# Layer-norm moments moved to ScalarE and the graph products started one tile earlier

## The reference

```python
xn = _layernorm(x)                       # (x - mean) / sqrt(var + 1e-5) over the 768 features of a token
x = x + gnn(xn, src, dst) + mix(xn)      # two graph attention layers; a linear-attention block with MLP
x = x + ffn(_layernorm(x))               # experts chosen by a router

# inside gnn
x_norm = layer_norm(xn, norm_g, norm_b)  # a second norm, of the normalised x
out1 = gat_conv(x_norm, src, dst, W1, ...)
out2 = gat_conv(out1, src, dst, W2, ...)
combined = concatenate([xn, out2], axis=-1)
return combined @ Wu + bu                # the first 768 rows of Wu meet xn itself
```

## Time and profile before

| what | us |
|---|---|
| median of 3 runs | 2093.31 |
| the profiled execution's own time | 2087.36 |
| its span (first to last instruction) | 2085.6 |
| PE busy | 1939.0 |
| DVE busy | 1163.6 |
| ACT busy | 624.6 |
| POOL busy | 423.9 |

### The profile page before, as it was taken

The page is one execution under the profiler, slowest core; times in us unless marked ns, Lnnn a source line. Parts: engine busy times, 40 slices in busy tenths (PEclk is TensorE's granted clock), DMA queues, the critical chain, the costliest instruction groups (busy, mean ns, idle before and its releaser), DMA issues.

```text
span 2085.6 us, 28329 instructions
## 1 busy us (share of the span) xinstructions
PE 1939.0 (93%) x10975; PEld 1836.1 (88%) x10975; DVE 1163.6 (56%) x2089; ACT 624.6 (30%) x1235; POOL 423.9 (20%) x323
## 2 busy tenths in 40 slices
PE   6799995999978899999899999999979999999995
PEld 3476895999878899888899999999969999999995
DVE  8977444888678332566743352442467344274347
ACT  2541323888677231222510010010241001010024
POOL 1000001011000233502242141330205123043120
PEclk9899997999979899999999999999989999999998
DMA  4231310111113321003321120110123011021013
GB/s 135 96 120 67 101 40 34 44 41 59 62 66 115 118 68 46 23 1 100 102 61 31 31 61 8 54 53 8 32 81 92 16 46 61 9 76 43 20 38 125
DMA packets 74476, 124.32 MB, mean 60 GB/s; under 512 B 3297, under 2 KB 45065, under 8 KB 74348
## 3 DMA queue, kind: packets, MB, share of 16 engines
q1 hardware_dynamic: 74348, 122.59, 18.2%
HBM read 97.12 MB, written 25.45 MB: 59 GB/s over the span
## 4 chain that ended last, share of the span: by engine, by line
PE 75%; DVE 8%; DMA 5%; ACT 4%; issue 3%; SPq 2%; POOL 1%; DVEq 0%; ACTq 0%; POOLq 0%
PE pb L964 24%; PE pa L603 23%; PE pb L603 11%; PE pb L755 4%; PE pb L872 2%; PE pa L742 2%; PE pa L755 2%; DMA md<-md_d 2%; PE pa L656 2%; DMA wt_d<-xu 2%; PE pb L773 1%; ACT sm L1309 1%; SPq L406 1%; DMA raw<-in_L_gnn_Wu 1%; ACT o1h L1334 1%
## 5 line engine op out<-in xcount | busy, mean ns | idle before, releaser
L1502 ACT ACTIVATE tr<-pb,V 128x418 f32<-128x418 f32 (+1 forms) x144 | 87.8, 610 | 769.1 <-PE pb L964 769.0
L964 PE MATMUL pb<-X_hi,uw_hi 128*128 128x416 f32 (+1 forms) x864 | 306.0, 354 | 6.0 <-issue 6.0
L964 PE MATMUL pb<-X_hi,uw_lo 128*128 128x416 f32 (+1 forms) x864 | 305.3, 353 | 0.0
L964 PE MATMUL pb<-X_lo,uw_hi 128*128 128x416 f32 (+1 forms) x864 | 305.3, 353 | 0.0
L603 PE MATMUL pa<-dw_hi,hh 128*125 128x384 f32 x960 | 246.4, 338 | 0.7 <-ACT tr L1502 0.7
L603 PE MATMUL pa<-dw_hi,hl 128*125 128x384 f32 x960 | 246.0, 337 | 0.0
L603 PE MATMUL pa<-dw_lo,hh 128*125 128x384 f32 x960 | 245.9, 337 | 0.0
L1968 DVE CAST hh<-tr 128x418 fp32r<-128x418 f32 (+1 forms) x144 | 115.3, 801 | 221.8 <-ACT tr L1502 221.8
L1082 POOL CAST uw_hi<-raw 128x768 fp32r<-128x768 f32 x48 | 42.5, 885 | 702.9 <-PE pb L964 611.6
L603 PEld LDWEIGHTS pa<-dw_hi,hh 128*125 128x125 f32 x960 | 172.4, 185 | 1.1 <-ACT tr L1502 1.0
L603 PEld LDWEIGHTS pa<-dw_lo,hh 128*125 128x125 f32 x960 | 172.9, 185 | 0.0
(11 more groups left out here) (359 smaller groups left out, 3581.5 us busy)
## 6 DMA issues: line engine op xcount, KB each, us to landing
raw<-in_L_mix_fc_w SPq DMA_DIRECT2D x48, 384.0 KB, 3.3
raw<-in_L_ffn_w SPq DMA_DIRECT2D x48, 384.0 KB, 3.3
md<-md_d SPq DMA_DIRECT2D x20, 610.4 KB
md_d<-mds SPq DMA_DIRECT2D x10, 610.4 KB
raw<-in_L_mix_qkv_w SPq DMA_DIRECT2D x24, 192.0 KB, 5.1
TOK<-in_x SPq DMA_DIRECT2D x10, 375.0 KB
xn_d<-TOK SPq DMA_DIRECT2D x10, 375.0 KB
xu<-in_x SPq DMA_DIRECT2D x10, 375.0 KB
```

The source lines that it names most:

```text
L964: last = nc.tensor.matmul(pb[:, j % 4, 0:n], w_[:, kk, :], x_[:, kk, o:o + n], start=(kk == 0 and q == 0), stop=(kk == KT - 1 and q == 2))
L1502: last = A_(RE[f"tr{j % 3}"][:, 0:w], pb[:, j % 4, 0:w], ACT.Identity if func == "mish" else func, bias=bias(b))
```

## The change

The moments of token tiles 0 to 5 are taken on ScalarE (`moments_of`: tiles 0 and 1 before the loop, 2 and 3 in t = 0, 4 and 5 in t = 1), by sums as in `spread_of`. VectorE takes those of tiles 6 to 9, two each in t = 4 and t = 5. The norms are now made for tiles 0 to 3 in t = 1, for 4 and 5 in t = 3, and for 6 to 9 in t = 6; the second norm's scales follow in t = 7 and 8 instead of 4 and 5. XFIRST goes from 3 to 2: transposes begin in t = 2, products in t = 3, and after tile 9 two token tiles are left instead of three. Only tile 1's sums are in `pb`. The edit, cut to its core:

```diff
-XFIRST = 3
+XFIRST = 2
+X_LOADS = ((0, 1, 2, 3), (4, 5, 6, 7), (8, 9))
+ACT_MOMENTS = 6
 def ln_tiles(t):
-    return {1: (0, 1, 2, 3), 2: (4, 5, 6, 7), 3: (8, 9)}.get(t, ())
+    return {1: (0, 1, 2, 3), 3: (4, 5), 6: (6, 7, 8, 9)}.get(t, ())
         def edge_sums(t):
-            return pb if t in (1, XFIRST) else pa
+            return pb if t == 1 else pa
 # SyncE
-                for u in ln_tiles(t - 1):
+                for u in ln_tiles(t):
                     sp.wait_ge(*at("ln_xn", u + 1))
                     sp.dma_start(xn_d[u], TOK[:, u, :]).then_inc(sem("xn_out"), 16)
             for u in range(NT - XFIRST - 2, NT):
                 graph_tile(u)
-                for k in {NT - 5: (3, 4), NT - 4: (5,)}.get(u, ()):
+                for k in {NT - XFIRST - 2: (3, 4), NT - XFIRST - 1: (5,)}.get(u, ()):
 # TensorE, edge_counts
-                    pe.wait_ge(*at("e_sb", t - 1 if t <= XFIRST + 1 else t))
+                    pe.wait_ge(*at("e_sb", t - 1 if t <= XFIRST else t))
 # ScalarE
+            def moments_of(u):
+                junk = RE["c0"][:]
+                act.wait_ge(*at(*x_landed(u)))
+                ch.link(A_(junk, TOK[:, u, :], ACT.Copy, accum_out=st[:, u, 0, 0:1]))
+                ch.link(A_(mv[:, u, 0:1], st[:, u, 0, 0:1], ACT.Copy, scale=-1.0 / D))
+                ch.link(A_(junk, TOK[:, u, :], ACT.Square, bias=mv[:, u, 0:1], accum_out=st[:, u, 0, 1:2]))
+                A_(mv[:, u, 1:2], st[:, u, 0, 1:2], ACT.Copy, scale=1.0 / D).then_inc(sem("ln_mv"), 1)
+            for u in range(2):
+                moments_of(u)
             for k in range(3):
                 page_high(PG_WU + k, wu[k][0], func=ACT.Copy)
 ...
+                for u in {0: (2, 3), 1: (4, 5)}.get(t, ()):
+                    moments_of(u)
                 if t == 1:
                     for k in range(3, KT):
                         page_high(PG_WU + k, wu[k][0], func=ACT.Copy)
-            x_out(NT - 3)
+            x_out(NT - 2)
 # VectorE, the loop
-                if ln_tiles(t - 1):
-                    token_norms(t - 1)
+                if ln_tiles(t):
+                    token_norms(t)
                 for k in {0: (0, 1, 2), 2: (3, 4, 5)}.get(t, ()):
                     page_low(PG_WU + k, wu[k])
-                if ln_tiles(t):
-                    dve.wait_ge(*at(f"x_in{t - 1}", 16 * len(ln_tiles(t))))
-                    token_moments(t)
-                if t == 4:
+                if t in (4, 5):
+                    token_moments((2 * t - 2, 2 * t - 1))
+                if t == 7:
 ...
-                if t == 5:
+                if t == 8:
 # VectorE, after the loop
-            x_low(NT - 4)
+            x_low(NT - 3)
             edge_table(NT - 1)
-            x_low(NT - 3)
             gained_page(0)
             gained_page(1)
-            graph_rows(NT - 5)
+            graph_rows(NT - 4)
             x_low(NT - 2)
```

More of the change, by code:

```diff
@@ L124, in chunk_of, with ln_group, x_landed @@
     return max(c for c, (a, n) in enumerate(CHUNKS) if a <= last)
-XFIRST = 3
+XFIRST = 2
 def x_tiles(t):
     return (t - XFIRST,) if t >= XFIRST else ()
+X_LOADS = ((0, 1, 2, 3), (4, 5, 6, 7), (8, 9))
+ACT_MOMENTS = 6
 def ln_tiles(t):
-    return {1: (0, 1, 2, 3), 2: (4, 5, 6, 7), 3: (8, 9)}.get(t, ())
+    return {1: (0, 1, 2, 3), 3: (4, 5), 6: (6, 7, 8, 9)}.get(t, ())
+def ln_group(t):
+    return len([s for s in range(t + 1) if ln_tiles(s)])
+def x_landed(u):
+    n = [u in g for g in X_LOADS].index(True)
+    return f"x_in{n}", 16 * len(X_LOADS[n])
 def step_of(i):
@@ L404, in _ @@
             for n in range(3):
-                for t in ln_tiles(n + 1):
+                for t in X_LOADS[n]:
                     sp.dma_start(TOK[:, t, :], x_t[t]).then_inc(sem(f"x_in{n}"), 16)
@@ L667, in x_transposes @@
                 else:
-                    pe.wait_ge(*at("e_sb", XFIRST + 1))
+                    pe.wait_ge(*at("e_sb", XFIRST))
                 six_transposes(pb[:, 3, :], pb[:, 2, :], TOK[:, u, :]).then_inc(sem("x_tr"), 1)
@@ L1189, in _ @@
             A_ = nc.scalar.activation
+            ch = Chain(act, sem("act_chain"))
             act.wait_ge(*at("v_tr", 1))
@@ L1220, in _ @@
             for t in range(NT):
-                tiles = ln_tiles(t - 1)
+                tiles = ln_tiles(t)
                 if tiles:
                     a, b = tiles[0], tiles[-1] + 1
-                    act.wait_ge(*at("ln_ag", b))
+                    act.wait_ge(*(at("ln_mv", b) if b <= ACT_MOMENTS else at("ln_ag", b - ACT_MOMENTS)))
                     A_(ve[:, 0, a:b], mv[:, a:b, 1], ACT.Sqrt, bias=eps["eps5"]).then_inc(sem("ln_sd"), 1)
-                if t == 5:
+                if t == 8:
                     act.wait_ge(*at("ln_v", 1))
@@ L1242, in _ @@
                 if tiles:
-                    act.wait_ge(*at("ln_rs", t - 1))
+                    act.wait_ge(*at("ln_rs", ln_group(t)))
                     for u in tiles:
                         A_(TOK[:, u, :], TOK[:, u, :], ACT.Identity, scale=rs[:, 0, u:u + 1], bias=nm[:, u:u + 1]).then_inc(sem("ln_xn"), 1)
+                for u in {0: (2, 3), 1: (4, 5)}.get(t, ()):
+                    moments_of(u)
                 if t == 1:
@@ L1248, in _ @@
                         page_high(PG_WU + k, wu[k][0], func=ACT.Copy)
-            x_out(NT - 3)
+            x_out(NT - 2)
             for k in range(KT):
                 if k == 2:
-                    x_out(NT - 2)
                     for s in range(2):
@@ L1604, in one_hots, with token_moments @@
                                         ).then_inc(sem(f"oh{q}"), 1)
-            def token_moments(t):
-                for u in ln_tiles(t):
+            def token_moments(tiles):
+                for u in tiles:
+                    dve.wait_ge(*at(*x_landed(u)))
                     for k in range(2):
@@ L1616, in token_norms @@
                 a, b = tiles[0], tiles[-1] + 1
-                dve.wait_ge(*at("ln_ag", b))
-                dve.wait_ge(*at("ln_sd", t))
+                dve.wait_ge(*(at("ln_mv", b) if b <= ACT_MOMENTS else at("ln_ag", b - ACT_MOMENTS)))
+                dve.wait_ge(*at("ln_sd", ln_group(t)))
                 ch.link(v.reciprocal(rs[:, 0, a:b], ve[:, 0, a:b]))
-                v.scalar_tensor_tensor(out=nm[:, a:b], in0=mv[:, a:b, 0], scalar=-1.0, in1=rs[:, 0, a:b],
+                v.scalar_tensor_tensor(out=nm[:, a:b], in0=mv[:, a:b, 0], scalar=1.0 if b <= ACT_MOMENTS else -1.0, in1=rs[:, 0, a:b],
                                        op0=ALU.mult, op1=ALU.mult).then_inc(sem("ln_rs"), 1)
@@ L1691, in _ @@
             gained_page(2)
-            graph_rows(NT - 4)
+            graph_rows(NT - 3)
             x_low(NT - 1)
             gained_page(3)
-            graph_rows(NT - 3)
+            graph_rows(NT - 2)
             gained_page(4)
-            graph_rows(NT - 2)
             gained_page(5)
```

## The result

Before: 2092.36 us, the median of 20 runs (2085.87 to 2099.63). After: 2086.68 us, the median of 20 (2083.36 to 2089.91). The ratio is 0.9975, with a 95% interval of 0.9967 to 0.9982: 5.7 us faster by the medians, 5.2 by the ratio. A second comparison (e5) gave 0.998 (0.9971 to 0.9988): 4.2 us by the ratio, 2.8 by its medians. The execution profiled after took 2086.64 us, and its span is 2084.9 (before: 2087.36 and 2085.6). So the two profiled executions are 0.7 us apart, and the medians 5.7.

The account below looks back on a forecast made before the run. TensorE was taken as fullest, with VectorE and a Wu page setting the pace in front and SyncE's transfers behind. Terms +0.4 + 1.5 - 2.9 = -1.0 us gave 2092.3 on a median of 2093.31, no change, range 2087.8 to 2097.0.

Parts of the forecast that it names:

- Step 1: Tiles 1 to 3: tile 3's counts start 7.9 us earlier, at 66.8, held by the transfers of Wu's pages.
- Step 2: First product one tile earlier: tile 4's clearing starts at 87.8 instead of 92.08, -4.3 us.
- Step 3: Tiles 4 to 9: +4.7 us from moments and norms, TensorE gaps of 3.0, one slow clock +1.5; tile 9's clearing 199.4.
- Step 4: Behind tile 9: one product fewer, W1's pages still hold TensorE; second product with W1 at 266.1, -2.9 us.
- Sum: Whole kernel: +0.4 + 1.5 - 2.9 = -1.0 us, 2086.4 for the profiled execution, 2092.3 on the median.
- signs of being wrong: Wu's pages land at another time, TensorE doesn't stand still behind tile 9, or moments in tiles 4 and 5 disappear.
- signs of being right: Trace marks: split waits for a transfer near 59, step marks 66.8 and 87.8, 3 us gaps, 8 to 10 us idle.
- The pages of W1 don't hold the end: Rival, behind tile 9: `xu` writes return sooner, the end gives its whole 6.9 us; -5.0, 2088.3, chance 0.15.
- The gaps cost nothing: Rival, tiles 4 and 5: clock stays at 1.00, tile 3 takes 13.2 us; -3.0, 2090.3, chance 0.10.
- the two slower ones: Rivals: clock down through both products of tiles 4 and 5, 2100.8, chance 0.07; front gains less, 2095.3, chance 0.06.

Follow-up runs that it names:

- e5: The changed kernel again, no edit: 2087.61 us, ratio 0.998 to the kernel before.
- e6: The changed kernel with VectorE's moments of tiles 6 to 9 between the additions and the edge table in tiles 4 and 5: 2079.15 us, ratio 0.9944 to before.
- e1: The kernel before again, no edit, second profile: 2092.65 us, ratio 1.0005.
- e8: The kernel before again, no edit, third profile: 2091.86 us.
- e11: The kernel before again, no edit, fourth profile: 2097.5 us.
- e3: The changed kernel with VectorE's moments of tiles 6 to 9 last in t = 4 and 5, behind additions and edge table: 2087.42 us, ratio 0.9976 to before.
- e4: The changed kernel with W1's pages 3, 4 and 5 loaded one graph tile earlier: 2082.97 us, ratio 0.996 to before.
- e9: e6 with W1's pages 3, 4 and 5 issued one graph tile earlier, as in e4: 2075.05 us, ratio 0.9918 to before.
- e7: The changed kernel with XFIRST left at 3 and W1's pages 3, 4 and 5 issued one graph tile earlier: 2084.0 us, ratio 0.9971 to before.
- e12: The kernel before plus thrown-away TensorE products in two waits, ahead of tile 3's counts and of the first W1 product: 2091.0 us, ratio 0.9999.
- e13: The kernel before plus 42 thrown-away clearing products ahead of tile 3's counts alone: 2094.42 us, ratio 1.0015.

## Why the prediction was wrong

The marks of the steps held within 1.1 us, two of them by luck, and the base didn't hold. In the order of the prediction:

- **Step 1** (tile 3's counts at 66.8): 67.50. The last page's low part ends at 63.04 (62.8 was said); from the addition of `bu` to the count it is 67.50 - 62.95 = 4.55 us instead of 4.0, with 1.33 of issue in it. The wait behind this mark was not the one named. The pages' transfers no longer hold the split; ScalarE's moments of tiles 4 and 5 (4.7 us, up to 59.48) do, and they end 0.4 us behind the 59.09 that the transfers had set. That the two fall together is luck.
- **Step 2** (tile 4's clearing at 87.8): 88.89, 1.1 us late: 0.7 from step 1, and 0.4 from counts that took 14.06 us instead of 13.7.
- **Step 3** (waits of 3.0 us in tiles 4 and 5, one of two with a slow clock, tile 9's clearing 199.4 to 200.9): waits of 3.00 and 3.00, clock 1.00 behind the first and 0.76 behind the second, clearing at 200.19. The Trainium skill (TensorE: Matmul & The Clock Gate, HAM oscillation — how this bites in real kernels) has recurring waits put the engine back to half rate each time; these two equal waits, short beside those the page describes, did so once. The end of this step came out partly by luck: a tile without longer waits takes 20.7 us (e6), not 21.35, and the 1.3 us that this saves in tiles 4 and 5 is spent again on 1.19 of issue. Tiles 6 to 8 take 62.93 us instead of 64.05 + 0.6, which more than makes up for the late start of step 2.
- **Step 4** (TensorE idle 8 to 10 us ahead of page 3, 67 us from tile 9's clearing to the second product): 9.10 us; the second product follows at once on the first and starts at 267.39, and 267.39 - 200.19 = 67.2.
- **Sum** (-1.0 on the profiled execution's own time): 2087.36 to 2086.64, -0.7. None of the prediction's signs of being wrong came; of its signs of being right one is missing, the split's wait for a transfer.

The step that failed is the last sentence of the sum, "on the median of 2093.31 that is 2092.3". It takes for granted that a median execution of before is the profiled one with 5.95 us added in places that the change leaves alone. Of the miss of 5.6 us, 0.95 is the median itself (2093.31 of 3 runs, 2092.36 of 20); the rest goes with that premise. The profiles of both kernels, from TensorE's timelines, in us:

| | tile 9's clearing | dg | span |
|---|---|---|---|
| before, first profile | 199.05 | 281.71 | 2085.6 |
| before, e1, e8, e11 | 200.43, 200.58, 200.35 | 284.56, 283.65, 284.59 | 2090.5, 2090.1, 2095.7 |
| before, mean of four | 200.10 | 283.63 | 2090.5 |
| after, two profiles | 200.19, 200.29 | 280.01, 280.25 | 2084.9, 2086.3 |
| after, mean | 200.24 | 280.13 | 2085.6 |

Against the mean of four the stage ends 3.5 us earlier, against the three later ones 284.27 - 280.13 = 4.1. In them tile 4's counts start among short waits at a low clock, worth 1.4 us; the change puts a product there, and both its profiles have TensorE busy and the clock at 1.00 from 80 to 100 us. And the second product with W1, which takes 14.2 instead of 12.7 us to dg in two of four profiles of before, takes 12.6 in both of the changed kernel, where it no longer waits. In the profile that I read the first cost little and the second nothing.

The fifteen profiles of all kernels bear this out. Tile 4's counts take 11.76 us in each of the six with the earlier product (both of the change, e3, e4, e6, e9), and 12.51 to 14.27 in the nine without. From the second product with W1 to dg it is 14.1 to 14.3 us in four of the nine profiles where it waits 2.2 us or more (e1, e11, e4, e7) and 12.7 in the other five; in the six where it waits under 1 us it is never more than 12.71. So in all of them the earlier product does away with the slow stretch; and the slow product comes only behind a wait, but not behind each. Which of the waits about tile 4 slows its counts is not shown: the long one ahead of tile 3 isn't it (e12), and the short ones were not tried alone.

The remaining 1.4 of the 4.9 us between the mean spans lie behind the stage, in code that the change doesn't touch, where single profiles of before differ by 7 us from dg to the end (1803.9 to 1811.1), and the changed kernel's two (1804.9 and 1806.0) lie inside. About 1004 us, for instance, the first profile of before is fast and e11's is not:

```profile
1004.00:1014.00 10.00, 9.25 (x58) 9.22 (x59) 6.13 (x13) 4.10 (x9) 1.85 (x1) 1.00 0.32 118
```
```profile
1004.00:1014.00 10.00, 5.93 (x29) 5.61 (x28) 8.81 (x16) 7.40 (x21) 1.84 (x1) 0.75 0.23 79
```

Whether the change moves that part or two profiles are too few stays open.

Of the rivals, none was the case. "The pages of W1 don't hold the end" forecast 2088.3, nearest to the result, by a mechanism that isn't there: the pages did hold it (9.10 us, and e4 frees 3.8 of them). "The gaps cost nothing" was wrong for one of two. Of the two slower ones, the clock was back within both products, so the first did not come. (Its price of 5 us fits the rows: a pair of this product's matmuls takes 0.65 us at a clock of 0.50 and 0.36 at 1.00, 5.2 us on 6.4. The reason given for it doesn't show: the records of the weight loads lengthen as much as the pairs do, from 0.18 to 0.33 us each.) The second came in small: the front is 1.1 us late. Also missed by the prediction was what the moments' place costs in tile 5 beyond 2.16 and 1.5 us (1.19 of issue), and with it how cheap the cure is: e6 moves two lines by one statement and gains more than the change.

## What to carry to other kernels

A sum worked out in one trace is a difference to that execution; where its own time lies outside the timed runs (2087.36 beside 2089.74 to 2094.66), ask which of its stretches ran better than they usually do, and whether the change makes that luck certain. A second profile of the kernel before is worth more than a finer sum. When work moves off an engine's critical path, look for its place behind what the other engine waits for and ahead of what hides the next register loads: 7.5 us hung on that order here, more than on the change.

## What the hardware showed that I had not expected

- Loads of loop bounds into VectorE's registers can be long: 0.92 to 2.36 us each in e3 behind a short bn_aggr, with 4.19 and 6.12 us of idle time before a tile's one-hots, and 0.30 us each in e6, beside a table subtraction and with 0.69 us of idle time. What makes them so long is open: from 107 to 110 us the DMA engines were busy to 0.85, from 131 to 135 to 0.31.
- Equal waits, unequal clocks: two of 3.00 us in one kernel gave 1.00 and 0.76, and one of 2.3 to 2.6 us in before gave 12.7 us from the following product's start to dg in two profiles and 14.1 to 14.3 in two.
- Keeping TensorE at work through a wait of 10 us made the next counts faster (12.50 us in e12 and 13.21 in e13, instead of 13.6 to 14.2), and won nothing, as another engine set the pace.
